# A message-passing layer on one core: the turn, the copies and the next feature product placed some per cent of a block later

## The reference

```python
src_h = h[src] @ W_msg.T + b_msg
msg = src_h + edge_embed[clip(edge_type, 0, 8)]
messages = segment_sum(msg, dst, num_segments=12500)
h_new = gru_cell(messages, h, W_ih, W_hh, b_ih, b_hh)   # r, z: sigmoid; n: tanh
out = layernorm(h + h_new)
```

## Time and profile before

| | |
|---|---|
| time, median of 3 runs | 1085.25 us (1083.91 to 1088.41) |
| span of the profiled execution | 1255.1 us |
| PE busy | 1037.9 us (83%), 8411 matmuls |
| DVE / ACT / POOL busy | 859.2 / 660.5 / 733.5 us |
| mean granted clock of PE | 0.926 |

### The profile page before, as it was taken

How to read it: one execution, slowest core, us unless ns; L and a number is a source line. 1 busy time by engine, 2 the same in 40 slices (tenths; PEclk the granted TensorE clock), 3 DMA queues, 4 the chain that set the end, 5 groups by cost and what they waited for, 6 DMA issues and landing times.

```text
span 1255.1 us, 23526 instructions
## 1 busy us (share of the span) xinstructions
PE 1037.9 (83%) x8411; PEld 656.5 (52%) x8411; DVE 859.2 (68%) x2699; ACT 660.5 (53%) x1283; POOL 733.5 (58%) x779
## 2 busy tenths in 40 slices
PE   5456677888888988989889989889888888888884
PEld 2124354555555555556556656555555555555552
DVE  8413557677776877868777767777876777676644
ACT  4243404455655555656666656555655556554622
POOL 7725645665566666666666666566666666566640
PEclk9566568999999999999999999999998999999996
DMA  8529311222222322322333223223323233332321
GB/s 244 159 79 310 107 33 53 78 77 74 74 77 79 91 77 77 91 78 77 82 83 92 79 78 92 74 79 92 90 77 89 76 89 83 86 92 80 83 81 28
DMA packets 94565, 114.23 MB, mean 91 GB/s; under 512 B 19820, under 2 KB 80616, under 8 KB 94441
## 3 DMA queue, kind: packets, MB, share of 16 engines
q0 software_dynamic: 35264, 73.19, 21.8%
q1 hardware_dynamic: 57320, 37.79, 10.2%
q10 hardware_dynamic: 1856, 1.66, 0.5%
HBM read 96.56 MB, written 16.00 MB: 90 GB/s over the span
## 4 chain that ended last, share of the span: by engine, by line
PE 64%; issue 10%; DVE 9%; ACT 7%; another core or an unknown queue 7%; DMA 1%; SPq 1%; DVEq 0%; ACTq 0%
PE psf L1097 28%; PE psb L1082 14%; PE pAB L1026 5%; PE psg L1065 4%; PE pAB L1040 4%; ACT mem L1213 3%; DVE ohl L868 2%; PE pAB L1043 2%; DVE ohk L862 2%; PE psg L1069 2%; PE psf L1102 1%; DMA arena<-in_x 1%; ACT mem L1153 1%; DVE ohk L865 1%
## 5 line engine op out<-in xcount | busy, mean ns | idle before, releaser
L604 POOL DMA_INDIRECT xg<-x_split,idx x648 | 616.1, 951 | 392.1 <-PE psg L1069 151.0
L1213 ACT CAST mem<-psb 128x432 f16<-128x432 f32 x896 | 426.7, 525 | 398.4 <-PE psb L1082 300.8
L1097 PE MATMUL psf<-mem 128*128 128x384 bf16 (+1 forms) x2744 | 618.4, 330 | 13.6 <-issue 6.8
L1082 PE MATMUL psb<-ohk,ohl 128*128 128x108 bf16 (+3 forms) x1865 | 421.6, 264 | 97.9 <-issue 57.4
L862 DVE TENSOR_TENSOR ohk<-table_bank,prm 128x392 bf16<-128x392 f16 (+3 forms) x437 | 271.0, 620 | 108.6 <-PE psb L1082 69.1
L1097 PEld LDWEIGHTS psf<-mem 128*128 128x128 f16 (+1 forms) x2744 | 240.4, 99 | 131.3 <-issue 34.9
L1082 PEld LDWEIGHTS psb<-ohk,ohl 128*128 128x128 bf16 x1865 | 173.6, 100 | 251.3 <-issue 116.4
L868 DVE TENSOR_TENSOR ohl<-table_bank,prm 128x512 bf16<-128x512 f16 x437 | 180.8, 414 | 0.0
L891 DVE TENSOR_TENSOR mem<-mem,psg 128x136 f32 (+9 forms) x184 | 54.9, 298 | 168.4 <-remote 106.8
L604 POOL DMA_INDIRECT xg<-in_x,idx x88 | 84.2, 957 | 76.3 <-PE psg L1069 44.7
L865 DVE TENSOR_TENSOR ohk<-table_bank,sort 128x40 bf16<-128x40 f16 (+3 forms) x437 | 106.5, 244 | 0.0
(11 more groups left out here) (148 smaller groups left out, 808.4 us busy)
## 6 DMA issues: line engine op xcount, KB each, us to landing
xg<-x_split,idx POOLq DMA_INDIRECT x648
x_split<-mem SPq DMA_DIRECT2D x24, 384.0 KB
xb<-in_xT SPq DMA_DIRECT2D x49, 128.0 KB
arena<-in_x SPq DMA_DIRECT2D x24, 256.0 KB
arena<-in_xN SPq DMA_DIRECT2D x47, 128.0 KB
out<-spill SPq DMA_DIRECT2D x19, 128.0 KB
out<-arena SPq DMA_DIRECT2D x144, 8.0 KB
out<-arena SPq DMA_DIRECT2D x15, 128.0 KB
```

The costliest lines, as they stand in the source:

```text
L604: pool.indirect_dma_start(out=xg[:, p % RING, :] if split else xg32(p % RING), out_offset=None, in_=x_d if split else x, in_offset=bass.In ...
L1082: ins = pe.matmul(psb[:, bank % NB, held * HC:(held + m) * HC], ohl[:, e % KB, :], ohk[:, e % KB, d * HC:(d + m) * HC], start=(k == 0), st ...
L1097: pe.matmul(psf[:, 0:3 * H], Bb[q % 2][0:kk, HT + h, :], xs[0:kk, h, :, :].rearrange("p c f -> p (c f)"), start=(h == 0), stop=(h == HI - ...
L1213: act.copy(Bb[q % 2][:, :, n:n + MOST], psb[:, bank % NB, 0:MOST * HC].rearrange("p (d h) -> p h d", h=HC)).then_inc(S["s_eb"], 1)
```

## The change

Two constants change. `T` goes from share 0.06 to 0.09 of the block, `C` from 0.10 to 0.13, and the first `F` of the next block from 0.17 to 0.19. `S` stays at 0.02. No instruction is added or removed.

```diff
-SETTLED = (0.02, 0.06, 0.10)
-CLEAR = 0.17
+SETTLED = (0.02, 0.09, 0.13)
+CLEAR = 0.19
```

## The result

The changed kernel took 1093.9 us (median of 5, 1088.6 to 1095.45) beside 1084.02 us for before (1082.31 to 1088.41). The ratio is 1.0078 with a 95% interval of 1.0059 to 1.0096: slower, by 8.5 us. On another chip it was 1.0088 (1.0066 to 1.0111).

What follows compares the result with a forecast made beforehand. PE, busy for 1037.9 of 1255.1 us, was taken to bound the kernel. Terms at the block ends and last block summed to +5.6 us, reduced to +4.5 for what comes back: 1089.5 us, range 1080 to 1098.

Steps and rivals of the forecast that it cites:

- 14, 15, 19, 23: Block ends: a later cast ahead of the copies, +0.15 us each; at 23 a group comes between, +0.65; together +1.1.
- 20: Block 20's end: load and root run in the wait ahead of `T`; `T` to `F` falls from 2.65 to 1.21, -1.4 us.
- 16, 17, 21, 25: Block ends: a group or slower cast moves from between `T` and `C` into the wait ahead of `T`, -1.5 us.
- 0, 9, 10, 12, 18: Ends where `F` doesn't wait: one or two slots move into the wait ahead of `T`, -0.4 us together.
- one more slot in each end: At 27 block ends one more slot, taken from the stretch of `F`, saves 0.055 us each, -1.5 us.
- Step (b): Block ends: what precedes the copies on ACT changes, so `F` starts later or earlier; terms from +4.6 to -1.5 us.
- The allowance for what comes back: After late `F`: DVE and ACT get ahead, shortening later PE waits for casts; a fifth, +5.6 becomes +4.5 us.
- Step (d): Last block: the last group but four and a final block's `su` now stand ahead of `T`, -1.1 us.
- The rule on the drain: Table loads on ACT: about 1380 ns extra per switch would make the estimate +7.2 us; less than 1 chance in 50.
- The filled wait: Rival: PE's wait ahead of `T` is filled and nothing given back, 8.2 us less, 1077 us; chance 0.15.
- other limits take it all up: Rival: PE's larger waits in front of slots absorb late and early `F` alike, 1085 us; chance 0.2.
- The losses without the gains: Rival: DVE is too late at block ends for the gains; 11.5 us loss against 3.0 gain, 1094 us; chance 0.2.

Runs made afterwards that it cites:

- roots_ahead: Kernel before with the square root and its table load put ahead of the copies at blocks 13, 22 and 24: 1094.03 us, 1.0094 of before.
- changed_again: The changed kernel, no edit, run again: 1092.3 us beside 1083.95 for before, ratio 1.0088.
- copies_first_before: Kernel before with `C` put directly behind `T` in the order: 1078.23 us, 0.9949 of before.
- copies_first_again: Changed kernel with `C` put directly behind `T`, on a chip of 1084 us: 1079.99 us, 0.9959 of before.
- the halves: Kernel before with only `T` and `C` later (0.9961), or only the first `F` one slot later (1.0024 and 0.9999).
- before_third: Kernel before, no edit, profiled once more on a slow chip: 1.0003 of before, span 1253.3 us.
- copies_first_after: Changed kernel with `C` put directly behind `T`, on the chip of 1256 us: 0.9962 of before.

## Why the prediction was right, and what was mis-sized

The direction and, in the main, the mechanism held: `F` waits for copies that stand too late on ACT. 1093.9 us lies in the range of 1080 to 1098, but beyond the forecast's own 1086 to 1093, and the +4.5 us were 8.5 by the ratio. To see which terms were off, take the distance between the last count matmuls of neighbouring blocks in the changed kernel's trace, and the same in roots_ahead, less its own 1.6 us at blocks 13, 22 and 24 and its clock falls (1.3 to 1.7 us each). Its other ends have before's order. Over the 27 distances the changed kernel is 9.6 us longer (9.7 in changed_again). By the same measure copies_first_before comes out 5.7 us shorter and copies_first_again 4.0, where the times say 5.7 and 4.2, so this stand-in for before serves:

| term of the sum | said, us | measured, us |
|---|---|---|
| 22, 24, 13: load and root ahead of the copies | +4.6 | +3.9, of it 1.5 a clock fall |
| 8, 11: sigmoid and cast ahead | +3.1 | +0.95 |
| 1 to 7: a cast ahead | +2.7 | +6.1, of it 1.6 a clock fall |
| 14, 15, 19, 23 | +1.1 | +0.6 |
| 20 | -1.4 | -1.1 |
| 16, 17, 21, 25 | -1.5 | -0.2 |
| 0, 9, 10, 12, 18 | -0.4 | -0.6 |
| one more slot in each end | -1.5 | in the rows above |
| sum over the dense blocks | +6.7 | +9.6 |

That the losses come to 11.5 us, as said, is luck: 8.4 without the clock falls, for which no term stood. Of the gains, 4.8 without the last block, only 1.9 came.

*Step (b)*, the copies' place, is right in kind at most ends, and close in the distance from `T` to `F`: 2.76 and 2.93 at 22 and 24 (said 2.8), 2.07 at 13 (2.2), 1.15 at 14 and 15 (1.21), 1.76 at 23 (1.85), 1.59 at 5 (1.59), 1.05 at 25 (1.25). It is not close at 17 (1.47, said 1.21) and at 19 (2.06, said 1.21). Over the whole block it is mis-sized in these places:

- At block 11 `F` did start 1.4 us later within the end, but the stretch after it became 1.4 shorter: all of it came back.
- At block 2, priced +0.3, the whole distance grew by 3.1, while blocks 0, 1 and 3 together became 1.1 shorter. In the changed order the `su`, sigmoid and tanh of a final block stand ahead of `T`, and the copies behind the tanh:

```profile
223.38 0.92 PE L1043 MATMUL pAB<-emw,cnts 128*128 128x512 f32 x2
224.35 0.45 PE L1108 MATMUL psf<-ident,added 128*128 128x128 f32 x2
226.08 0.42 ACT L1193 ACTIVATE arena<-arena 128x256 f32<-128x256 f32 x1 [1.14 <-DVE arena L799]
```

  `T` starts 1.97 us after `S` ends, in roots_ahead 0.05. In copies_first_again block 2 keeps its 3.1 us. So this part of the loss is the turn's place, and an edit of the copies alone doesn't take it back.
- At 20 the table load came ahead of `T` by only 0.2 us.
- At 21 and 25 the gains became losses, +0.8 and +0.4. The prediction's "`S` isn't moved" is wrong there: in the new list `yt` of a final block stands ahead of `S`. DVE at block 21 of the changed kernel, where the last count matmul ends at 847.40:

```profile
847.26 0.42 DVE L806 TENSOR_TENSOR arena<-arena 128x256 f32<-128x256 f32 x1
847.71 0.42 DVE L807 TENSOR_TENSOR arena<-arena 128x256 f32<-128x256 f32 x1
848.16 0.43 DVE L808 SCALAR_TENSOR_TENSOR arena<-arena 128x256 f32<-128x256 f32 x1
848.51 0.55 DVE L903 TENSOR_REDUCE added<-psf 128x128 f32<-128x384 f32 x1
```

  `S` starts 1.1 us after the count matmuls end (1.35 at 25), where it is 0.1 us in roots_ahead with these three behind it. From `T` to `F` both ends came as forecast.

*The allowance for what comes back* (a fifth, 1.1 us off) has the right sign. The changed kernel and copies_first_again have the same order but for the copies, so the pair shows it. From a block's last count matmul to the first `F` the changed kernel takes 14.9 us more over the 27 ends. After eight of them the stretch up to the next block's last count matmul is shorter, by 4.4 us together: three tenths come back, 1.4 at block 11, nothing at 13 and 22. After the ends of 7 and 24 it is 1.6 and 1.5 longer, by a clock fall each. These two falls, 3.1 of the 9.6 us, are a term that the sum lacked; the gains missing at 21 and 25 are the other thing that it lacked. 14.9 - 4.4 + 3.1 makes 13.6, and the times of the two kernels are 13 to 14 us apart. The place where it came back is not the one named: PE's waits for casts are 9.0 us in both traces, those for one-hot tiles (`ohl`) 3.2 in the changed kernel and 6.0 in copies_first_again.

*Step (d)*, 1.1 us at the last block, isn't visible: from block 27's last count matmul to the end the changed kernel's two traces have 36.9 and 39.4 us, copies_first_again has 39.0, roots_ahead and copies_first_before, with the old order there, 39.8 and 39.4. The spread is larger than the term, and it stays open.

*The rule on the drain* after a table load did not apply in the changed kernel either: load from 883.85 to 885.13, root at 885.15, copies at 885.35.

*The rivals.* The filled wait failed: PE's wait in front of `T` fell only from 12.5 us in roots_ahead to 11.4, short of the 3 to 6 us of the forecast's signs, and `F` waits more. About half of the 23.4 us of the earlier trace rows was the chip. That other limits take it all up is what the halves show on the chips of 1256 and 1274 us (0.9961 to 1.0024), and is wrong where before takes 1084. The losses without the gains came nearest in size, at 1094, and its reason, DVE late at the block ends, is found at 21 and 25 (there by DVE's order). But the gains of 16, 17 and 20 were there (0.5, 0.9 and 1.1 us), and two clock falls that it did not have make up 3.1 us.

## What to carry to other kernels

When a copy out of PSUM stands between two PE stages that share a bank, put it in the copying engine's order directly behind the instruction that it waits for, whatever share of the stage the planner gives its producer: here that alone was worth 13 to 14 us on the changed kernel and 5.7 us on the one before. It doesn't help where the producer itself has been put behind other work, as at block 2. When shares of a stage are moved, compare every engine's order around the items that were not moved too: at two ends `S` fell behind `yt` though its share stayed. Count table loads in front of such a copy separately, and expect more than their own time where they lengthen an existing wait of PE (three of them, 1.6 us each with the root, cost 10 us here). And look whether profile and times come from the same kind of chip before taking waits from the one into a sum for the other.

## What the runs showed of the hardware

**A long wait of PE can cost 1.3 to 1.7 us on top of itself.** In the traces from chips of 1084 us PE's clock stays at 1.00 through the dense stretch, also across ends where PE waits up to 1.9 us for `F` (block 22 of the changed kernel) and across all ends of the two kernels with the copies first. It falls to the lower of its two levels for 3.4 us after block ends with waits of 2.26 and 2.04 us for `F` (blocks 7 and 24 of the changed kernel, in both of its traces), and in roots_ahead after waits of 2.33, 0.72 (following 1.25 ahead of `T`), 2.32 and 1.72 us. What sets the limit these waits do not show: 1.86 us passed in both traces of the changed kernel and 1.85 in copies_first_again (block 7), and 1.72 did not. The price is the lengthening of the stretch from the first `F` to the block's last count matmul, beside the kernel of the same order with the copies first. The first pair of `F` after block 24 in the changed kernel, where pairs take 0.48 or 0.49 us otherwise:

```profile
956.03 0.80 PE L1097 MATMUL psf<-mem 128*128 128x384 bf16 x2 [2.04 <-ACT arena L1223]
```

The Trainium skill (TensorE: Matmul & The Clock Gate, HAM oscillation — how this bites in real kernels) says that waits between bursts of matmuls can drop the clock. The traces agree in kind, but the waits that it tells of are longer than any here; at 2.33 us and less the fall came too, at 1.3 to 1.7 us a time.

**Chips differ by a sixth for this kernel**: 1084 us on at least two, 1256 and 1274 us on two others, each steady. On the slow ones PE waits 46.5 us with no name in front of slots (before_third; the row below), none of it in the changed kernel's trace above, and its clock falls 4 to 12 times in the dense stretch in the nine traces from such chips (4 in copies_first_after). 53 to 68 us of the difference lie ahead of the dense stretch already: block 0's last count matmul ends at 212 to 223 us, against 155 to 159. An edit of 8 us on a fast chip measured nothing there. What makes these chips slow was not found.

```profile
PE psb L1082 <- issue: 46.5, 62, 2.0
```
